# Moving the transpose of the hidden state's odd chunks behind the next step's even-chunk matmuls in a recurrent layer

## What is computed

```python
xi = jnp.einsum('btd,hd->bth', x, Wi) + bi

def step(h, xt):
    h_new = jnp.tanh(xt + h @ Wh.T + bh)
    return (h_new, h_new)
...
x = _layernorm(x + _L0_attn_ref(x, Wi, bi, Wh, bh), axis=-1)
x = _layernorm(x + _L0_ffn_ref(x, ...), axis=-1)   # router, 16 experts, top 4
```

## Time and profile before

| | us |
|---|---|
| median of 2 runs | 8033.28 |
| their range | 8026.66 to 8039.89 |
| the profiled execution, its own time | 7924.17 |
| its span on the slowest core (core 5) | 7922.5 |
| spans of the 8 cores | 7845.7 to 7922.5 |

### The profile page before, as it was taken

The page is one execution under the profiler, slowest core; times in us unless marked ns, Lnnn a source line. Parts: engine busy times, 40 slices in busy tenths (PEclk is TensorE's granted clock), DMA queues, the critical chain, the costliest instruction groups (busy, mean ns, idle before and its releaser), DMA issues. The chain is left out here.

```text
span 7922.5 us, 378438 instructions; the slowest of 8 cores (7845.7 to 7922.5 us)
## 1 busy us (share of the span) xinstructions
PE 5905.3 (75%) x170612; PEld 4244.3 (54%) x170612; DVE 1972.3 (25%) x9625; ACT 1248.5 (16%) x4381; POOL 44.2 (1%) x56
## 2 busy tenths in 40 slices
PE   5777777777777777777777777777771688888883
PEld 3666666666666666666666666666660233333331
DVE  1111111111111111111111111111116444444446
ACT  0111111111111111111111111111110000000000
POOL 0000000000000000000000000000000000000000
PEclk8777777777767777776776777767765899999996
DMA  3000000000000000000000000000001211111101
GB/s 48 4 4 4 4 4 4 4 4 4 4 4 4 4 4 4 4 4 4 4 4 4 4 4 4 4 4 4 4 5 41 48 33 33 33 32 32 33 17 43
DMA packets 51106, 100.45 MB, mean 13 GB/s; under 512 B 2919, under 2 KB 36200, under 8 KB 47482
## 3 DMA queue, kind: packets, MB, share of 16 engines
q0 software_dynamic: 45888, 58.76, 4.6%
q1 hardware_dynamic: 3642, 17.48, 0.6%
HBM read 126.59 MB, written 8.39 MB: 17 GB/s over the span
## 5 line engine op out<-in xcount | busy, mean ns | idle before, releaser
L183 DVE CAST hstat<-tpA 128x4 f16<-128x4 f32 x2048 | 333.0, 163 | 4590.1 <-PE tpA L228 4590.1
L246 ACT ACTIVATE hsp<-zA 128x128 f16<-128x128 f32 x2048 | 568.5, 278 | 4497.3 <-PE zA L220 4497.3
L211 PE MATMUL zA<-whT,hstat 128*32 128x128 f16 x32768 | 1182.5, 274 | 75.2 <-issue 73.6
L211 PE MATMUL zB<-whT,hstat 128*32 128x128 f16 x32768 | 1154.9, 268 | 82.7 <-issue 81.5
L220 PE MATMUL zB<-whT,hstat 128*32 128x128 f16 x32768 | 1132.7, 264 | 73.7 <-issue 73.2
L220 PE MATMUL zA<-whT,hstat 128*32 128x128 f16 x32768 | 1127.4, 264 | 69.6 <-issue 68.5
L211 PEld LDWEIGHTS zA<-whT,hstat 128*32 128x32 f16 x32768 | 851.1, 127 | 107.2 <-issue 104.2
L211 PEld LDWEIGHTS zB<-whT,hstat 128*32 128x32 f16 x32768 | 842.1, 125 | 112.8 <-issue 111.3
L220 PEld LDWEIGHTS zB<-whT,hstat 128*32 128x32 f16 x32768 | 815.9, 121 | 100.7 <-issue 99.4
L220 PEld LDWEIGHTS zA<-whT,hstat 128*32 128x32 f16 x32768 | 813.3, 122 | 95.6 <-issue 94.7
L203 PE MATMUL zA<-xi_stream,id_sb 128*32 128x128 f16 x8192 | 571.0, 259 | 374.1 <-DVE buf_h L184 283.2
(11 more groups left out here) (123 smaller groups left out, 3105.3 us busy)
## 6 DMA issues: line engine op xcount, KB each, us to landing
wg<-gpT POOLq DMA_DIRECT2D x16, 1024.0 KB, 9.4
wu<-upT POOLq DMA_DIRECT2D x16, 1024.0 KB, 13.6
wd<-dpT POOLq DMA_DIRECT2D x16, 1024.0 KB, 17.7
xbuf<-x_fm SPq DMA_DIRECT2D x8, 1024.0 KB, 5.0
outT<-och SPq DMA_DIRECT2D x8, 1024.0 KB, 3.9
x<-x_fm POOLq DMA_DIRECT2D x1, 4096.0 KB, 33.9
wiT<-wiT POOLq DMA_DIRECT2D x1, 2048.0 KB, 45.7
whT<-whT POOLq DMA_DIRECT2D x1, 2048.0 KB, 54.6
```

What stands on the lines that cost most here:

```text
L183: v.tensor_copy(out=hstat[:, hs:hs + 4], in_=tpA[par][:, :])
L211: te.matmul(out=zb_[par][32 * g:32 * g + 32, 0:128], lhsT=bass.AP(hstat, par * 8 + COLOF(kc), [[16, 128], [0, 32]]), rhs=whT16[:, kc * D + ...
L246: sc.activation(out=hsp[:, par * 256:par * 256 + 128], in_=zA[par][:, 0:128], func=AF.Tanh).then_inc(s_th, 1)
```

## The change

The four matmuls that write tpB, with their wait for `s_th1`, become a helper `transp_w1(t)`. It is no longer called at the end of step t but inside step t+1, between the even-chunk matmuls (L211) and the wait for `s_ev1` ahead of the odd-chunk ones (L220). For the last step it is called once behind the loop. PE therefore goes from tpA of step t straight to the wait for `s_ev` and the xi matmuls of step t+1. What is computed, the number of instructions, the buffers, and the programs of ACT and DVE stay the same.

```diff
--- before.py
+++ after.py
@@ -191,6 +191,17 @@
                 @blk.tensor
                 def _(te):
                     halves = [(zA, 0), (zB, 128)]
+
+                    def transp_w1(t):
+                        par = t % 2
+                        te.wait_ge(s_th1, t + 1)
+                        for j in range(4):
+                            ti = te.matmul(out=tpB[par][32 * j:32 * j + 32, 0:4],
+                                           lhsT=hsp[:, par * 256 + 128 + 32 * j: par * 256 + 128 + 32 * j + 32],
+                                           rhs=sel_sb[:, :], start=True, stop=True,
+                                           tile_position=(0, 32 * j))
+                        ti.then_inc(s_tr1, 1)
+
                     for t in range(t_steps):
                         par = t % 2
                         blkofs = (t // 128) * D
@@ -213,6 +224,8 @@
                                               rhs=whT16[:, kc * D + 256 * g + ofs: kc * D + 256 * g + ofs + 128],
                                               start=False, stop=False, tile_position=(0, 32 * g),
                                               skip_group_check=True)
+                        if t >= 1:
+                            transp_w1(t - 1)
                         te.wait_ge(s_ev1, t + 1)
                         for zb_, ofs, s_done in [(zA, 0, s_mm), (zB, 128, s_mm1)]:
                             for kc in range(1, KC, 2):
@@ -230,13 +243,7 @@
                                            rhs=sel_sb[:, :], start=True, stop=True,
                                            tile_position=(0, 32 * j))
                         ti.then_inc(s_tr, 1)
-                        te.wait_ge(s_th1, t + 1)
-                        for j in range(4):
-                            ti = te.matmul(out=tpB[par][32 * j:32 * j + 32, 0:4],
-                                           lhsT=hsp[:, par * 256 + 128 + 32 * j: par * 256 + 128 + 32 * j + 32],
-                                           rhs=sel_sb[:, :], start=True, stop=True,
-                                           tile_position=(0, 32 * j))
-                        ti.then_inc(s_tr1, 1)
+                    transp_w1(t_steps - 1)
 
                 @blk.scalar
                 def _(sc):
```

## The result

| | before | after |
|---|---|---|
| median, us | 8033.58 (10 runs) | 9777.8 (11 runs) |
| range, us | 7919.29 to 8159.52 | 9633.96 to 9840.81 |
| recurrence, first to last tpA, slowest core | 5813.7 | 7518.3 |
| the same, a step (divided by 2047) | 2.840 | 3.673 |

What follows compares the result with a forecast made beforehand. The prediction took the PE, ACT, PE, DVE, PE round trip as the bound: 3.54 us a step at 1.2 GHz plus 0.07 stalls, times 2048, is +1578 on 7922.5, 9500; half of 109 added gives 9555 us, range 9350 to 9800.

Steps and rivals of the forecast that it cites:

- What bounds it: Recurrence, 2048 steps of 2.84 us: no engine is full; a round trip between engines sets the end.
- the gain of nothing: Between tpA and xi: s_ev sets the 0.69 us, so taking tpB away gains 0 to 28 us, taken as 0.
- the ring: Each step's round trip PE, ACT, PE, DVE, PE: 2.90 us at 1.2 GHz, 2.18 at 2.4.
- The cover that is gone: Ahead of the odd matmuls: tpB's trip through DVE, before under xi and the even matmuls, now adds 0.69 us a step.
- the trip: From tpB through DVE's cast and copy to the odd matmuls: taken as 0.69 us, bounds 0.54 plus semaphore to 0.74.
- The refund: First four odd matmuls, now starting after a wait: 0.05 us a step back at 1.2 GHz, nothing at 2.4.
- The level: PE clock in the recurrence: falls within the first steps and stays at 1.2 GHz; chance 0.84.
- Code stalls: PE's "issue" idle in the dense matmul groups: 0 to 0.14 us a step, half taken, 0.07.
- The sum: Whole span: 3.61 us x 2048 = 7393 against 5815, +1578 on 7922.5, giving 9500 us.
- The median: Over the runs: half of the 109 us between median and profiled execution added to the span, giving 9555 us.
- The one with the clock's mix kept: Rival for the recurrence: clock levels stay mixed, only the trip is paid, about 9185 us; chance 0.10.
- The one at 2.4 GHz throughout: Rival for the recurrence: warm clock, 2.87 us a step, 5878 us, median about 8040, not slower; chance 0.04.

Runs made afterwards that it cites:

- e6: Kernel before, with s_ev and s_ev1 signalled by DVE's casts instead of the copies behind them; median 7898.82 us, ratio 0.9935 to before.
- e4: Kernel before plus two unused 384-column matmuls a step, ahead of tpA and of xi; 8077.16 us beside 8012.17 for before.
- e7: Kernel before with the 8 xi matmuls ahead of the wait for s_ev instead of behind it; median 7979.17 us, ratio 0.9898 to before.
- e9: Kernel before with the edits of e6 and e7 together; median 7833.87 us, ratio 0.9853 to before.
- e1: Changed kernel with tpB moved to right behind xi, ahead of all 32 even matmuls; 8336.17 us beside 8012.17 for the kernel before.
- e2: Changed kernel with tpB moved between the 16 even matmuls of zA and the 16 of zB; 8841.5 us beside 8012.17 for the kernel before.
- e5: Changed kernel with s_ev and s_ev1 signalled by DVE's casts instead of the copies behind them; recurrence 7215.6 us against 7518.3.
- e3: Changed kernel plus five unused 384-column matmuls a step in PE's gaps; 8944.99 us, recurrence 6595.6 us against 7518.3.
- e10: e4 plus 16 more already-reached semaphore waits a step on PE, behind the wait for s_ev1; 11146.0 us, one run.
- e13: Changed kernel with each group of four 32-column transposing matmuls made one of 128 columns; recurrence 7547.0 us against 7518.3.

## Why the prediction was right, and what was off

**What bounds it, and the gain of nothing.** Right for the changed kernel: tpA to xi is 0.69 after as before; tpB had stood in the shadow of the DVE trip. e6 shows how thin the shadow was at 1.2 GHz, 0.03. Not right is the sentence that only what lengthens or shortens the ring counts: in the kernel before, the supply of code held the mean step at 2.8 (e4, e7, e9), and a shorter ring gained little (67 us in e9). The forecast didn't suffer, because a step of 3.63 is far above what the code allows; that was luck as much as insight.

**The cover that is gone.** Right in kind: e1, e2 and the changed kernel give the exposed part in three doses, and e5 takes 0.07 off at the new wait. Off in size: the trip was put at 0.69 with 0.74 as its upper bound, and measured 0.77. The copied row was tpA's, which starts on an idle PE: tpB's four matmuls now take 0.25 instead of 0.20, and the cast starts 0.39 behind them instead of 0.31 (3002.89 to 3003.28, against 3001.18 to 3001.49 for tpA in the same step). Behind a running stream of matmuls at 1.2 GHz such a trip is longer by 0.08. This is 0.08 x 2048 = 164 us, all of the miss in the clean step but for rounding: 3.63 against 3.54. Why it is longer there isn't tested.

**The refund.** Right: the odd group to the next tpA takes 1.15 instead of 1.19.

**The level.** Right: 0.50 throughout, from the first steps on. e3 adds what the forecast had only as a guess, that the level depends on what PE does in its gaps: five idle-time matmuls a step brought back 0.99. The rule of the Trainium skill that the prediction set against this (TensorE: Matmul & The Clock Gate, "Why this matters for your kernels"), that it is long idle gaps between bursts that cost the warm clock in mid-kernel, isn't borne out: no idle time of PE in this recurrence is over 0.9 us, and it stays at 0.50.

**Code stalls.** Put at 0.07 a step; what stands above the clean step is 3.673 - 3.63 = 0.04, a small error to the other side, 0.03 x 2048 = 61 us. That the two are near each other is luck: PE has no idle time put down to "issue" in its dense groups any more, so the stalls that were meant are 0, and the 0.04 is something else. In the step that starts at 3004.81, for one, DVE begins the copy of tpA 0.24 late and xi follows tpA after 1.02. The 0.14 a step taken for the kernel before was too small as well: by the prediction's own 44% of the time at 2.4 GHz the clean steps 2.18 and 2.90 give a mean of 1 / (0.44 / 2.18 + 0.56 / 2.90) = 2.53, which leaves 0.31 of the 2.84. The forecast took half of the 0.14 into its step, the rivals more.

**The sum.** 9500 was forecast for the span on a core that the stages behind don't slow, and 9628.9 is the shortest after. The difference of 129 is (3.673 - 3.61) x 2048: 0.09 more in the clean step, 0.03 less above it.

**The median.** 9555 against 9777.8. Half of the 109 us between the median and the profiled execution of before was added, on the guess that the mix of clock levels made it and would go. It was a wrong guess: the offset of the median from an undisturbed span is 9777.8 - 9628.9 = 149 us after, 94 more than the 55 added, and with the 129 above this is the whole miss of 223. In the profiled execution the recurrence took the same 7518 to 7521 us on all eight cores; what differs between them is the clock in the stages behind it. The core that ended last had 0.80 there (7700 to 9790 above, 2090 us), core 0 of the same execution 0.89 and 150 us less:

```profile
7700.00:9640.00 1940.00, 1485.59 (x6482) 599.50 (x6482) 974.23 (x1376) 166.65 (x284) 40.32 (x48) 0.89 0.18 32
```

**The rivals.** The one with the clock's mix kept didn't come; e1, whose exposed part is small, is the kernel that keeps a mix (0.69). The one at 2.4 GHz throughout had the right step for a wrong price: 2.87 clean, where e3 has 2.89, but 5878 us for the recurrence where e3 has 6596. It left the code stalls out of its sum. At 1.2 GHz they do vanish behind the longer step; at 2.4 GHz they were 3.222 - 2.89 = 0.33 a step. So this rival would not have been "not slower" either: 6596 against 5814.

## What to carry to other kernels

In a recurrence, ask of every step of the ring what lies over it, and move an instruction only if its consumer's cover moves with it: here the transposes left a gap in which they were free and went behind the very matmuls that hid their way back. Price a wait twice, once in its own time and once in the clock: of 1705 us lost, 922 came back with the clock. And before shortening a ring, look at the idle time put down to "issue": where the code of an unrolled loop comes late, as it did here at 2.8 us a step, fewer instructions gain more than a shorter chain (324 us for 12 of 165 instructions, 67 for the shorter ring of e9).

## What the hardware showed that was not expected

- Warming the clock of the kernel before from 0.72 to 0.98 was worth 10 of 5773 us (medians over the eight cores). The "issue" idle in its dense matmul groups grew from 297 to 667 us instead, and 1181 of 1182 stalls of e4 end 1.1 to 1.8 us behind the landing of a 16 KB packet of code.
- A semaphore wait on a value long reached costs PE 61 to 101 ns when many stand in a row: 17 of them were a gap of 1.03 us, and a clean step at 2.4 GHz grew by 1.61 (e10).
- The round trip of a transpose through DVE is 0.69 us from an idle PE and 0.77 behind a stream of matmuls at 1.2 GHz (0.70 to 0.71 at 2.4 GHz, e1 and e3).
- One transposing matmul with 128 stationary columns does the work of four with 32. At 1.2 GHz the time to its consumer is 0.04 us shorter from an idle PE; behind a stream it starts 0.17 later and is then 0.10 shorter, 0.07 more in all (e13).
